# Four transformer layers on one core: normalised rows written on VectorE, a retimed small-head attention, and extra matmuls at its start

## The chip, the cores and the metric

The kernel runs on one core of a Trainium2 chip, as one launch. The metric is the device time of that launch in microseconds (us). TensorE (PE in the rows; PEld is its weight load), VectorE (DVE), ScalarE (ACT), GpSimd (POOL) and SyncE (SP, which only issues DMAs here) run side by side and wait for each other through semaphores. Each engine takes its own instructions strictly in program order.

## The reference

A state x of 16 sequences, 256 tokens and 128 channels passes through four attention and four feed-forward parts. After each part the state is added and normalised over the channels:

```python
x = _layernorm(x + _L0_attn_ref(x, ...))   # 16 heads of 64, inner norm
x = _layernorm(x + _L0_ffn_ref(x, ...))    # top-1 experts, fixed capacity
x = _layernorm(x + _L1_attn_ref(x, ...))   # softmax(-distance(q, k)), 16 heads of 8
x = _layernorm(x + _L1_ffn_ref(x, ...))    # top-2 experts, one mean weight per expert
x = _layernorm(x + _L2_attn_ref(x, ...))   # grouped projections, 16 heads of 8
x = _layernorm(x + _L2_ffn_ref(x, ...))    # MLP with weights +1 and -1
x = _layernorm(x + _L3_attn_ref(x, ...))   # causal, 16 heads of 8
x = _layernorm(x + _L3_ffn_ref(x, ...))    # top-2 experts with capacity, and a shared one
```

In `_L1_ffn_ref` each expert's output is multiplied by `mean_w`, the mean of the pair weights of the tokens that chose it, so it is one number for an expert. `_L2_attn_ref` and `_L3_attn_ref` are ordinary softmax attention with 8 channels a head; the third layer's is causal.

## The kernel before

The whole state stays on chip in `x_state` (128 partitions, 32 tiles of 128 channels); a batch is one sequence, that is two tiles (`TB` = 2), and there are 16 batches. The eight parts run one after another with a barrier between them. Three functions matter here:

- `attention_wide` is layer 0, `attention_dist` is layer 1, and `attention_small` is run twice, for layer 2 (not causal) and for layer 3 (causal).
- `routed_layer` is the expert part of layers 0, 1 and 3. It leaves its rows in a DRAM tensor, `results`. The attention of the next layer fetches them ("get", GpSimd indirect DMAs, one for a tile and expert), adds them to x ("join"), takes the moments ("stats"), forms 1/sqrt(var + eps) on GpSimd ("root") and writes the normalised rows into `x_state` (`write_last`).
- `sign_mlp` is the feed-forward part of layer 2. It leaves its sum on chip, so that layer 3's attention has no gathers; its join is one GpSimd addition (`join_acc`).

All attention functions share one schedule: a loop over slots, written out by hand in every engine's program. Slot s starts head s of the 256 (16 batches of 16 heads). Work on batch b is placed at an offset: `at(s, X_AT)` is true in slot 16 b + X_AT. Slots are only an order of instructions on each engine. In a slot of `attention_small` TensorE does `score(s)` (one head's scores, into one of two PSUM banks), then `score_turned(s - 30)` (the same scores transposed, with the negated maximum of each row added by three extra rows), then, twice in four slots, `weigh` (four heads' probabilities times values). VectorE does `row_max(s)`; the score of head n waits until the maximum of head n - 2 is taken. ScalarE does `exps(s - 30)`.

Around that, once a batch: X_AT = -35 transposes x, QK_AT = -33 projects q and k, `split_qk` (GpSimd) cuts them into three bf16 parts, V_AT = -29 projects v and starts `stack` on SyncE (two stores to DRAM, then six loads that spread the parts over partitions for all 16 heads). `score` of a batch's first head waits for these loads. After the last head come `turn_o` (slots OT_AT = 54 to 57), `normalise`, `turn_on`, `project_out` (Y_AT = 63), `norm_stats`, `root_var`, `write_x` and then `turn_new`, which transposes the finished rows (F_AT).

In the kernel before, `attention_small` gets its rows far ahead (GET_AT = X_AT - 35), joins at X_AT - 18, takes stats at X_AT - 17 and roots at X_AT - 15. Both normalised writes, `write_last` and `write_x`, are ScalarE activations, and as these take scale and bias, GpSimd also forms shift = -mean times rstd (two more small instructions, lines 674/676 and 701/703):

```python
nc.gpsimd.tensor_tensor(rstd[:], veps[:], mhalf[:], ALU.pow)
nc.gpsimd.tensor_tensor(shift[:], mv[:, :, 0], rstd[:], ALU.mult)
nc.gpsimd.tensor_scalar(shift[:], shift[:], -1.0, None, ALU.mult)
```

In `attention_dist`, `write_x` is two GpSimd instructions right behind the root (line 1231). In layer 1's `routed_layer` the mean weight of an expert is applied to each tile of rows as it leaves PSUM (`tile_mean`, line 2153), so that the join of layer 2 is two plain additions of 256 elements (line 1004).

Of the kernel before, what the change touches and what calls it, by code (L numbers as in the profile page):

```python
# [9 lines left out]
ALU = mybir.AluOpType  # L10
# [489 lines left out]
def attention_small(nc, name, x_state, consts, w, scratch, scale, causal, last, onward):  # L500
# [22 lines left out]
    with ExitStack() as ctx:  # L523
# [23 lines left out]
        shift, lshift = sb("shift", [P, TB]), sb("lshift", [P, 2, TB])  # L547
# [22 lines left out]
        JOINED = max(K, 1)  # L570
# [28 lines left out]
        with nc.Block() as block:  # L599
# [28 lines left out]
            def _(pool):  # L628
# [38 lines left out]
                def root_var(b):  # L667
                    pool.wait_ge(y_steps, 5 * (b + 1))
                    after(pool, x_done, TB * b)
                    nc.gpsimd.tensor_scalar(veps[:], mv[:, :, 1], EPS, None, ALU.add).then_inc(rooted, 1)  # L670
                    pool.wait_ge(rooted, 4 * b + 1)
                    nc.gpsimd.tensor_tensor(rstd[:], veps[:], mhalf[:], ALU.pow).then_inc(rooted, 1)
                    pool.wait_ge(rooted, 4 * b + 2)
                    nc.gpsimd.tensor_tensor(shift[:], mv[:, :, 0], rstd[:], ALU.mult).then_inc(rooted, 1)
                    pool.wait_ge(rooted, 4 * b + 3)
                    nc.gpsimd.tensor_scalar(shift[:], shift[:], -1.0, None, ALU.mult).then_inc(rooted, 1)
# [17 lines left out]
                def root_last(b):  # L694
# [3 lines left out]
                    pool.wait_ge(l_rooted, 4 * b + 1)  # L698
                    nc.gpsimd.tensor_tensor(lrstd[:, b % 2, :], lveps[:, b % 2, :], mhalf[:], ALU.pow).then_inc(l_rooted, 1)
                    pool.wait_ge(l_rooted, 4 * b + 2)  # L700
                    nc.gpsimd.tensor_tensor(lshift[:, b % 2, :], lmv[:, b % 2, :, 0], lrstd[:, b % 2, :], ALU.mult).then_inc(l_rooted, 1)
                    pool.wait_ge(l_rooted, 4 * b + 3)
                    nc.gpsimd.tensor_scalar(lshift[:, b % 2, :], lshift[:, b % 2, :], -1.0, None, ALU.mult).then_inc(l_rooted, 1)

                for s in range(FIRST, LAST + 4):
# [9 lines left out]
                    if (b := at(s, Y_AT + 4)) is not None:  # L715
                        root_var(b)
# [4 lines left out]
                    if (b := at(s, OT_AT - 4)) is not None:  # L721
                        add_out_bias(b)

            @block.tensor
            def _(pe):
                pe.wait_ge(loaded, LOADED)

# [114 lines left out]
                for s in range(FIRST, LAST + 4):  # L842
# [29 lines left out]
            def _(act):  # L872
# [46 lines left out]
                def write_last(b):  # L919
                    act.wait_ge(l_rooted, 4 * b + 4)  # L920
                    for tile in range(TB):
                        nc.scalar.activation(x_state[:, TB * b + tile, :], ly(b)[:, tile, :], ACT.Identity, bias=lshift[:, b % 2, tile:tile + 1],
                                             scale=lrstd[:, b % 2, tile:tile + 1]).then_inc(x_ready, 1)

                def write_x(b):
                    act.wait_ge(rooted, 4 * b + 4)
                    for t in range(TB):
                        nc.scalar.activation(x_state[:, TB * b + t, :], y[:, t, :], ACT.Identity, bias=shift[:, t:t + 1], scale=rstd[:, t:t + 1]).then_inc(x_done, 1)

# [27 lines left out]
            def _(dve):  # L957
# [40 lines left out]

                def join_rows(b):
                    dve.wait_ge(fetched[b % 2], 16 * TB * K * (b // 2 + 1))  # L1000
                    after(dve, x_ready, TB * (b - 1))
                    for k in range(K):
                        after(dve, joined_x, K * b + k if k else 0)
                        nc.vector.tensor_tensor(ly(b), lrows[:, b % 2, :, k, :], ly(b) if k else x_state[:, TB * b:TB * (b + 1), :], ALU.add).then_inc(joined_x, 1)
# [14 lines left out]
                for s in range(FIRST, LAST + 9):  # L1019
                    if K and (b := at(s, JOIN_AT)) is not None:  # L1020
                        join_rows(b)
                    if (b := at(s, STATS_AT)) is not None:
                        stats_last(b)
                    if (n := head(s)) is not None:
# [7 lines left out]
                    if onward["gate"] is not None and (b := at(s, LG_AT)) is not None:  # L1032
# [3 lines left out]
def attention_dist(nc, name, x_state, consts, w, scratch, last, onward):  # L1036
# [24 lines left out]
    with ExitStack() as ctx:  # L1061
# [85 lines left out]
        with nc.Block() as block:  # L1147
# [37 lines left out]
            def _(pool):  # L1185
# [42 lines left out]
                def write_x(b):  # L1228
                    pool.wait_ge(rooted_var, 2 * b + 2)
                    for t in range(TB):  # L1230
                        nc.gpsimd.tensor_scalar(x_state[:, TB * b + t, :], y[:, t, :], mv[:, t, 0:1], rstd[:, t:t + 1],
                                                ALU.subtract, ALU.mult).then_inc(x_done, 1)

# [28 lines left out]
                for s in range(FIRST, LAST + 8):  # L1262
# [16 lines left out]
                    if (b := at(s, Y_AT + 3)) is not None:  # L1279
                        root_var(b)  # L1280
                        write_x(b)
# [247 lines left out]
            def _(dve):  # L1529
# [52 lines left out]

                def stats_last(b):
# [12 lines left out]
                for s in range(FIRST, LAST + 8):  # L1596
# [12 lines left out]
                    if (b := at(s, Y_AT + 2)) is not None:  # L1609
                        norm_stats(b)  # L1610


def routed_layer(nc, layer, x_state, consts, w, dram, held, XT):
# [17 lines left out]
    with ExitStack() as ctx:  # L1631
# [60 lines left out]
        if mean2:  # L1692
            wsum, mean, silus = sb("wsum", [P, E]), sb("mean", [P, E]), sb("silus", [P, 2, F])
            tile_mean, meant = sb("tile_mean", [P, Q]), sem("meant")
# [49 lines left out]
        with nc.Block() as block:  # L1744
# [226 lines left out]
            def _(dve):  # L1971
# [109 lines left out]
                def mean_weights():  # L2081
# [4 lines left out]
                    link(nc.vector.tensor_tensor(past[:], numbers[:, 0:E].unsqueeze(1).to_broadcast([P, Q, E]),  # L2086
                                                 tile_of[:].unsqueeze(2).to_broadcast([P, Q, E]), ALU.is_equal))
                    link(nc.vector.tensor_tensor(past[:], past[:], mean[:].unsqueeze(1).to_broadcast([P, Q, E]), ALU.mult))
# [421 lines left out]
```

## Time and profile before

| | |
|---|---|
| median of 3 runs | 2958.49 us (2956.53 to 2959.1) |
| the profiled execution | 2959.1 us, of which the span of instructions is 2957.3 us |
| busy share of the span | PE 80%, PEld 56%, DVE 49%, ACT 50%, POOL 45% |
| mean granted TensorE clock | 0.875 of full |
| layer 2 attention, first to last write | 1641.6 to 2043.4 us |
| layer 3 attention, first to last write | about 2231 to 2582.6 us |

The granted clock has two levels, 0.50 (1.2 GHz) and 1.00 (2.4 GHz); a window with a value between them holds some of both. Times of instructions are counted in us from the first instruction. The profile is of one execution, so its own time, 2959.1 us, is the one that the rows add up to.

### The profile page before, as it was taken

The page shows a single profiled execution, that of the slowest core. Times are in us where ns is not written, and L with a number is a line of the kernel's source. Part 1 is how long each engine was busy: PE and PEld are TensorE (multiplying, and loading weights), DVE is VectorE, ACT ScalarE, POOL GpSimd, SP SyncE. Part 2 cuts the span into 40 slices and gives each one's busy share as a digit, 9 for nine tenths or more (in the row PEclk, how much of TensorE's full clock was granted, in tenths as well). Part 3 has the DMA queues.
Part 4 walks back from the last instruction along what each step waited for, and adds up shares of the span by engine and source line. Part 5 has one row for each costly group of instructions (what it writes and reads, how often), then busy time and mean ns, then how long its engine had stood idle before and what let it go on. Part 6 is the DMA issues. An engine that isn't in the chain of part 4 may idle for free. (4 is left out here: it accounts for less than half of the span.)

```text
span 2957.3 us, 52459 instructions
## 1 busy us (share of the span) xinstructions
PE 2353.9 (80%) x17870; PEld 1649.4 (56%) x17870; DVE 1451.2 (49%) x4042; ACT 1478.2 (50%) x3688; POOL 1331.2 (45%) x2068
## 2 busy tenths in 40 slices
PE   6999999994667999970699499996996999835860
PEld 4666666663654666540699245553553777524750
DVE  3555555553116999962233356672003566330753
ACT  4666666662336999960122146674221666511421
POOL 2444444444227888635433546531003454253255
PEclk9999999997776999995799558898995999977975
DMA  3000000002113222103111233320002322020212
GB/s 135 1 1 1 1 1 1 1 1 77 64 56 96 73 73 72 50 8 118 50 44 48 81 94 86 90 69 8 0 0 75 105 89 88 4 73 32 80 64 61
DMA packets 100387, 153.42 MB, mean 52 GB/s; under 512 B 16850, under 2 KB 69988, under 8 KB 93092
## 3 DMA queue, kind: packets, MB, share of 16 engines
q1 hardware_dynamic: 88356, 128.32, 13.7%
q0 software_dynamic: 11776, 21.81, 2.4%
q8 instruction: 146, 2.39, 0.3%
q14 instruction: 109, 0.89, 0.1%
HBM read 99.85 MB, written 48.24 MB: 50 GB/s over the span
## 5 line engine op out<-in xcount | busy, mean ns | idle before, releaser
L970 DVE TENSOR_REDUCE A_nmax<-A_S 128x2 f32<-128x512 f32 (+1 forms) x512 | 310.5, 621 | 227.8 <-PE A_S L760 110.6
L181 POOL TENSOR_SCALAR A_prob<-A_prob,A_rinv 128x256 f32<-128x256 f32 x512 | 235.4, 478 | 371.1 <-DVE A_rinv L433 371.1
L901 ACT ACTIVATE A_PT<-A_E 128x512 f32<-128x512 f32 (+1 forms) x512 | 275.3, 546 | 163.9 <-PE A_E L777 78.9
L428 DVE TENSOR_REDUCE A_nmax<-A_S 128x2 f32<-128x512 f32 x256 | 164.8, 685 | 160.9 <-PE A_S L271 160.9
L371 ACT ACTIVATE A_prob<-A_S,A_nmax 128x256 f32<-128x256 f32 x512 | 234.8, 477 | 4.9 <-DVE A_nmax L428 4.9
L1787 POOL COPY L_wr<-L_w 128x1024 f32 (+1 forms) x144 | 104.1, 725 | 242.5 <-PE L_k L1861 125.5
L1780 POOL DMA_INDIRECT sent<-x_state,row x160 | 154.6, 966 | 118.5 <-DVEq L2036 70.7
L1552 DVE TENSOR_SCALAR_CACHE_REDUCE A_D<-A_S 128x256 f32<-128x256 f32 x512 | 193.5, 417 | 16.8 <-PE A_S L1335 16.6
L1558 DVE COPY A_PT<-A_T 128x512 f32<-128x512 f32 x256 | 175.2, 687 | 19.3 <-PE A_T L1348 18.8
L1348 PE MATMUL A_T<-ident_sb,A_D 128*128 128x128 f32 x1024 | 161.3, 281 | 27.1 <-ACT A_D L1477 14.5
L1954 ACT ACTIVATE L_silus<-L_k 128x512 f32<-128x512 f32 x72 | 43.0, 597 | 262.7 <-PE L_k L1857 262.7
L1871 PE MATMUL L_k<-L_w,L_hT 128*128 (+1 forms) x1184 | 162.7, 275 | 0.8 <-ACT L_hT L1959 0.7
L254 PE MATMUL A_M<-A_xT,A_wqk 128*128 128x256 f32 x512 | 143.5, 403 | 22.3 <-ACT A_xT L357 16.2
L793 PE MATMUL A_O<-A_PT,A_v 128*32 128x256 f32 (+1 forms) x2048 | 160.4, 387 | 0.0
L384 ACT ACTIVATE A_OT<-A_O,A_bv 128x256 f32<-128x256 f32 x128 | 60.6, 474 | 191.0 <-PE A_O L299 191.0
L1348 PEld LDWEIGHTS A_T<-ident_sb,A_D 128*128 128x128 f32 x1024 | 117.5, 143 | 56.8 <-ACT A_D L1477 22.7
L1871 PEld LDWEIGHTS L_k<-L_w,L_hT 128*128 128x128 f32 x1184 | 147.0, 192 | 1.6 <-issue 1.1
L1840 PE MATMUL L_k<-ident_sb,L_xe 128*128 128x128 f32 x184 | 29.3, 287 | 147.2 <-DMA L_xe<-sent 146.2
L271 PE MATMUL A_S<-A_QK 64*128 64x256 f32 x1024 | 146.1, 404 | 0.0
L1213 POOL TENSOR_TENSOR A_D<-A_D 128x1024 f32<-128x1024 f32 x64 | 120.7, 1892 | 47.5 <-ACT A_D L1472 47.3
L299 PE MATMUL A_O<-A_PT,A_V 128*64 128x256 f32 x1024 | 138.8, 392 | 0.8 <-ACT logit L394 0.8
L284 PEld LDWEIGHTS A_T<-ident_sb,A_prob 128*128 128x128 f32 x1024 | 117.4, 141 | 37.2 <-issue 34.5
(380 smaller groups left out, 6024.2 us busy)
## 6 DMA issues: line engine op xcount, KB each, us to landing
A_QS<-stack_q SPq DMA_DIRECT2D x144, 192.0 KB
A_KS<-stack_k SPq DMA_DIRECT2D x144, 192.0 KB
L_xe<-sent SPq DMA_DIRECT2D x46, 256.0 KB
results<-L_ye SPq DMA_DIRECT2D x46, 256.0 KB
stack_q<-A_parts SPq DMA_DIRECT2D x48, 192.0 KB
stack_k<-A_parts SPq DMA_DIRECT2D x48, 192.0 KB
L_w<-f_w SPq DMA_DIRECT2D x24, 256.0 KB, 10.4
sent<-A_zeros SPq DMA_DIRECT2D x9, 512.0 KB
```

Of the source, the lines that this page charges most:

```text
L181: nc.gpsimd.tensor_scalar(prob[:, n % NP, j, t, :], prob[:, n % NP, j, t, :], rinv[:, n % NP, j, t:t + 1], 1.0, ALU.mult, ALU.mult).then_i ...
L271: i = nc.tensor.matmul(psS[n % 2][j][:, t, :], QK[rows, n % NQ, 0, t * P:(t + 1) * P], QK[rows, n % NQ, 1, :], start=True, stop=True)
L371: nc.scalar.activation(prob[:, n % NP, j, t, :], psS[n % 2][j][:, t, :], ACT.Exp, bias=nmax[:, n % NP, j, t:t + 1], scale=1.0, accum_out=r ...
L428: nc.vector.tensor_reduce(nmax[:, n % NP, j, :], psS[n % 2][j][:], AX.X, ALU.max, negate=True).then_inc(maxed, 1)
L793: i = nc.tensor.matmul(psO[32 * j:32 * (j + 1), 0, n0:], v1[:, b % NV, m, h, :], p, start=(m == 0), stop=(m == TB - 1), skip_group_check=True)
L901: nc.scalar.activation(PT[:, n % RING, :], psE[n % 2][:, 0:BLOCKS, :].rearrange("p a b -> p (a b)"), ACT.Exp, scale=scale).then_inc(expd, 1)
L970: nc.vector.tensor_reduce(nmax[:, b % 2, :, h], view, AX.X, ALU.max, negate=True).then_inc(maxed, 1)
L1348: i = nc.tensor.transpose(T[:, m, t * P:(t + 1) * P], D[:, u % RD, c:c + P], consts["ident"][:])
L1552: nc.vector.tensor_scalar(D[:, u % RD, c:c + SEQ], psS[n % 2][:, t, :], 1e-12, None, ALU.max, ALU.min, accum_out=D[:, u % RD, W + TB * j + ...
L1558: nc.vector.tensor_copy(PT[:, n % RP], psT[n % 2][:]).then_inc(turned_v, 1)
L1780: pool.indirect_dma_start(sent, bass.IndirectOffsetOnAxis(ap=row[:, k, t:t + 1], axis=0), x_state[:, t, :], None).then_inc(sent_all, 16)
L1871: m = nc.tensor.matmul(psY[q % 2][:, k * P:(k + 1) * P], hT[:, i % HT, f, :], moving, start=(f == 0), stop=(f == NF - 1))
```

## The change

Five things are changed, and the rest is left alone:

1. In `attention_small` both normalised writes move from ScalarE to VectorE, as (y - mean) times rstd in one instruction a tile; the two shift instructions are gone from both roots on GpSimd.
2. The offsets of `attention_small` change: get X_AT - 19, join X_AT - 8, stats X_AT - 7, root X_AT - 5 in layer 2 (join X_AT - 15, stats X_AT - 10 in layer 3), `turn_new` two slots earlier, logits one.
3. TensorE gets `keep_busy`: a bf16 matmul of identity by identity, 128 x 128 weights and 512 columns, into a PSUM bank that nobody reads then: one in each slot from -8 to 29, four in each slot from 30 to 33. That is 54 in each of layers 2 and 3.
4. Layer 1's expert weight is no longer applied to the tiles; it is put into `weight` for each token and pair, and the join of layer 2 becomes four VectorE instructions (row times weight plus sum, 128 elements each) in place of two additions.
5. In `attention_dist` `write_x` moves from GpSimd to VectorE, four slots later.

```diff
-    F_AT, LG_AT = Y_AT + 11, Y_AT + 13
+    F_AT, LG_AT = Y_AT + 9, Y_AT + 12
-    GET_AT, NORM_AT = X_AT - 35, X_AT - 15
-    JOIN_AT, STATS_AT = (X_AT - 18, X_AT - 17) if last["K"] else (X_AT - 21, X_AT - 17)
+    GET_AT, NORM_AT = X_AT - 19, X_AT - 5
+    JOIN_AT, STATS_AT = (X_AT - 8, X_AT - 7) if last["K"] else (X_AT - 15, X_AT - 10)
-        JOINED = max(K, 1)
+        JOINED = TB * K if K else 1
 # attention_small, GpSimd: root_var (root_last likewise)
-                    nc.gpsimd.tensor_tensor(shift[:], mv[:, :, 0], rstd[:], ALU.mult).then_inc(rooted, 1)
-                    nc.gpsimd.tensor_scalar(shift[:], shift[:], -1.0, None, ALU.mult).then_inc(rooted, 1)
-                    if (b := at(s, Y_AT + 4)) is not None:
-                        root_var(b)
...
+                    if (b := at(s, Y_AT + 3)) is not None:
+                        root_var(b)
 # attention_small, TensorE
+                def keep_busy(times):
+                    for _ in range(times):
+                        nc.tensor.matmul(psB[:], consts["identb"][:], consts["identb"][:].unsqueeze(1).to_broadcast([P, 4, P]),
+                                         start=True, stop=True, skip_group_check=True)
...
+                    if -8 <= s < LAG_E:
+                        keep_busy(1)
+                    if LAG_E <= s < LAG_E + 4:
+                        keep_busy(4)
 # attention_small, ScalarE
-                def write_last(b):
-                    act.wait_ge(l_rooted, 4 * b + 4)
-                    for tile in range(TB):
-                        nc.scalar.activation(x_state[:, TB * b + tile, :], ly(b)[:, tile, :], ACT.Identity, bias=lshift[...], scale=lrstd[...])
-                def write_x(b): ...
-                    if (b := at(s, NORM_AT + 4)) is not None:
-                        write_last(b)
-                    if (b := at(s, Y_AT + 9)) is not None:
-                        write_x(b)
 # attention_small, VectorE (write_last the same with lmv, lrstd)
+                def write_x(b):
+                    dve.wait_ge(rooted, 2 * b + 2)
+                    for t in range(TB):
+                        nc.vector.tensor_scalar(x_state[:, TB * b + t, :], y[:, t, :], mv[:, t, 0:1], rstd[:, t:t + 1],
+                                                ALU.subtract, ALU.mult).then_inc(x_done, 1)
-                        nc.vector.tensor_tensor(ly(b), lrows[:, b % 2, :, k, :], ly(b) if k else x_state[...], ALU.add).then_inc(joined_x, 1)
+                        for tile in range(TB):
+                            nc.vector.scalar_tensor_tensor(out=ly(b)[:, tile, :], in0=lrows[:, b % 2, tile, k, :],
+                                                           scalar=last["weight"][...], in1=ly(b)[:, tile, :] if k else x_state[...],
+                                                           op0=ALU.mult, op1=ALU.add).then_inc(joined_x, 1)
+                    if (b := at(s, NORM_AT + 2)) is not None:
+                        write_last(b)
+                    if (b := at(s, Y_AT + 8)) is not None:
+                        write_x(b)
 # attention_dist: write_x leaves GpSimd (behind root_var at Y_AT + 3), VectorE gets
+                    if (b := at(s, Y_AT + 7)) is not None:
+                        write_x(b)
 # routed_layer of layer 1, VectorE: mean_weights and take_y
-                    link(nc.vector.tensor_tensor(past[:], numbers[...], tile_of[...], ALU.is_equal))
-                    link(nc.vector.tensor_tensor(past[:], past[:], mean[...], ALU.mult))
-                    nc.vector.tensor_reduce(tile_mean[:], past[:], AX.X, ALU.add).then_inc(meant, 1)
+                    for k, sel in enumerate((sel1, sel2)):
+                        link(nc.vector.tensor_tensor(d[:], sel[:], over_t(mean), ALU.mult))
+                        link(nc.vector.tensor_reduce(weight[:, k, :], d[:], AX.X, ALU.add))
-                        i = nc.vector.tensor_tensor(ye[...], by_tile(psY[q % 2]), tile_mean[...], ALU.mult)
+                        i = nc.vector.tensor_copy(ye[:, q % 2, :, :], by_tile(psY[q % 2]))
```

## Rows read from the trace of the kernel before

**Rows 1.** The page, part 2: granted TensorE clock in 40 equal slices.

```profile
PEclk9999999997776999995799558898995999977975
```

**Rows 2.** Windows: length; busy (count) of PE, PEld, DVE, ACT, POOL; clock; DMA; GB/s.

```profile
1718.40:1771.90 53.50, 53.50 (x278) 27.87 (x277) 25.33 (x48) 26.35 (x56) 21.62 (x35) 0.50 0.30 92
...
1806.90:1902.50 95.60, 88.05 (x660) 49.52 (x660) 58.48 (x130) 60.77 (x137) 52.61 (x96) 0.82 0.29 84
...
2264.40:2294.00 29.60, 27.59 (x160) 18.32 (x160) 18.54 (x41) 6.10 (x17) 12.76 (x23) 0.50 0.35 108
...
2327.00:2509.00 182.00, 182.00 (x2227) 138.78 (x2225) 110.54 (x301) 120.69 (x314) 88.77 (x180) 1.00 0.30 92
...
958.30:1252.40 294.10, 271.52 (x2400) 180.88 (x2396) 282.89 (x1137) 293.06 (x510) 234.79 (x259) 1.00 0.23 68
```

**Rows 3.** Windows of `row_max` (line 970), layers 2 and 3: its busy time, count, clock.

```profile
1702.70:1718.40 15.70, 10.57 (x16) 0.50 0.38 119
1718.40:1771.90 53.50, 22.02 (x32) 0.50 0.30 92
...
1771.90:1806.90 35.00, 18.64 (x28) 0.99 0.35 94
...
1895.70:1902.50 6.80, 3.37 (x5) 0.50 0.22 77
1902.50:1939.50 37.00, 20.50 (x31) 1.00 0.31 88
...
2327.00:2509.00 182.00, 86.74 (x159) 1.00 0.30 92
```

**Rows 4.** Timeline of TensorE, two stretches of layer 2: start, duration, line.

```profile
1719.58 0.63 PE L763 MATMUL A_S<-A_KS,A_QS 72*128 72x256 bf16 x2
...
1720.43 0.63 PE L763 MATMUL A_S<-A_KS,A_QS 72*128 72x256 bf16 x2
...
1923.99 0.39 PE L763 MATMUL A_S<-A_KS,A_QS 72*128 72x256 bf16 x2
...
1924.45 0.38 PE L763 MATMUL A_S<-A_KS,A_QS 72*128 72x256 bf16 x2
```

**Rows 5.** Timeline of layer 2, a join on VectorE and TensorE behind it.

```profile
1935.18 0.42 DVE L1004 TENSOR_TENSOR A_lsum<-A_lrows,A_lsum 128x256 f32<-128x256 f32 x1
...
1936.27 0.39 PE L763 MATMUL A_S<-A_KS,A_QS 72*128 72x256 bf16 x2 [0.82 <-DVE A_nmax L970]
```

**Rows 6.** Timeline, four other stretches: row writes and weighted additions by engine.

```profile
122.59 0.60 DVE L477 TENSOR_SCALAR x_state<-A_s,A_mv,A_rstd 128x128 f32<-128x128 f32 x2 [0.89 <-POOL A_rstd L196]
...
1321.10 1.58 POOL L1231 TENSOR_SCALAR x_state<-A_y,A_mv,A_rstd 128x128 f32<-128x128 f32 x2
...
2041.75 0.88 ACT L928 ACTIVATE x_state<-A_y,A_shift,A_rstd 128x128 f32<-128x128 f32 x2 [4.19 <-POOL A_shift L676]
...
2857.80 2.32 DVE L2168 SCALAR_TENSOR_TENSOR L_y<-L_rows,weight,L_y 128x128 f32<-128x128 f32 x8
```

**Rows 7.** Timeline, start of layer 2 attention.

```profile
1654.51 0.30 DVE L1013 BATCH_NORM_AGGREGATE A_lmv<-A_lstats 128x2 f32<-128x6 f32 x2
...
1656.95 0.27 POOL L697 TENSOR_SCALAR A_lveps<-A_lmv 128x2 f32<-128x2 f32 x1
...
1658.38 0.25 POOL L703 TENSOR_SCALAR A_lshift<-A_lshift 128x2 f32<-128x2 f32 x1
...
1658.76 0.88 ACT L922 ACTIVATE x_state<-A_lsum,A_lshift,A_lrstd 128x128 f32<-128x128 f32 x2 [15.92 <-POOL A_lshift L703]
...
1660.18 0.95 POOL L687 DMA_INDIRECT A_lrows<-results,row  x1 [0.30 <-issue]
...
1663.03 0.84 ACT L886 ACTIVATE A_qk<-A_X,A_bqk 128x256 f32<-128x256 f32 x2 [2.17 <-PE A_X L740]
...
1665.28 0.77 POOL L640 CAST A_parts<-A_qk 128x512 bf16<-128x512 f32 x1
```

**Rows 8.** Groups of VectorE by line and form in 958.3 to 1252.4.

```profile
L1568 DVE TENSOR_TENSOR A_On<-A_B,A_rinv 128x128 f32<-128x128 f32 x12 | 3.5, 292 | 0.4
```

More of the change, by code:

```diff
@@ L917, in take_max @@
                     nc.scalar.activation(nmT[:, b % 2, :], psA[:].rearrange("p a b -> p (a b)").bitcast(BF16)[0:PARTS * H, 0:SEQ], ACT.Copy).then_inc(nm_ready, 1)
-                def write_last(b):
-                    act.wait_ge(l_rooted, 4 * b + 4)
-                    for tile in range(TB):
[L922 to L928, printed above, removed]
                 def take_new(b):
@@ L1002, in join_rows, with write_last @@
                     for k in range(K):
-                        after(dve, joined_x, K * b + k if k else 0)
-                        nc.vector.tensor_tensor(ly(b), lrows[:, b % 2, :, k, :], ly(b) if k else x_state[:, TB * b:TB * (b + 1), :], ALU.add).then_inc(joined_x, 1)
+                        after(dve, joined_x, JOINED * b + TB * k if k else 0)
+                        for tile in range(TB):
+                            nc.vector.scalar_tensor_tensor(out=ly(b)[:, tile, :], in0=lrows[:, b % 2, tile, k, :],
+                                                           scalar=last["weight"][:, k, TB * b + tile:TB * b + tile + 1],
+                                                           in1=ly(b)[:, tile, :] if k else x_state[:, TB * b + tile, :],
+                                                           op0=ALU.mult, op1=ALU.add).then_inc(joined_x, 1)
+                def write_last(b):
+                    dve.wait_ge(l_rooted, 2 * b + 2)
+                    for tile in range(TB):
+                        nc.vector.tensor_scalar(x_state[:, TB * b + tile, :], ly(b)[:, tile, :], lmv[:, b % 2, tile, 0:1], lrstd[:, b % 2, tile:tile + 1],
+                                                ALU.subtract, ALU.mult).then_inc(x_ready, 1)
                 def stats_last(b):
@@ L1031, in _ @@
                         norm_stats(b)
-                    if onward["gate"] is not None and (b := at(s, LG_AT)) is not None:
+                    if (b := at(s, Y_AT + 8)) is not None:
+                        write_x(b)
+                    if onward["gate"] is not None and (b := at(s, LG_AT + 1)) is not None:
                         take_logits(b)
@@ L1226, in root_var @@
                     nc.gpsimd.tensor_tensor(rstd[:], veps[:], mhalf[:], ALU.pow).then_inc(rooted_var, 1)
[L1228 to L1232, printed above, removed]
                 def get_last(b, i):
@@ L1280, in _ @@
                         root_var(b)
-                        write_x(b)
             @block.tensor
@@ L1581, in norm_stats, with write_x @@
                         nc.vector.bn_aggr(mv[:, t, :], stats[:, t, :]).then_inc(y_steps, 1)
+                def write_x(b):
+                    dve.wait_ge(rooted_var, 2 * b + 2)
+                    for t in range(TB):
+                        nc.vector.tensor_scalar(x_state[:, TB * b + t, :], y[:, t, :], mv[:, t, 0:1], rstd[:, t:t + 1],
+                                                ALU.subtract, ALU.mult).then_inc(x_done, 1)
                 def stats_last(b):
```

19 lines of the change are left out of this document (2 added, 17 removed).

## The prediction

> **What bounds the kernel now.** I read four views, from the whole to one slot. The clock line of the page [rows 1] comes first: outside feed-forward parts TensorE is at full clock in most slices, but not where layer 2's attention runs (1641.6 to 2043.4, its slices 23 to 28) nor where layer 3's begins. The windows [rows 2] say what a low clock costs there. In 1718.4 to 1771.9 TensorE is busy for 53.50 of 53.50 us at 0.50: it is the bound, and at half speed. The windows of `row_max` [rows 3] count heads, one for each: 32 heads in those 53.5 us, 1.67 each, against 28 in 35.0 and 31 in 37.0 at full clock, 1.22 on the mean. Layer 3, full clock without a break and TensorE busy 182.00 of 182.00 [rows 2], has 159 heads in 182.0 [rows 3], 1.145 a head or 18.3 a batch. Between 1806.9 and 1902.5 the clock falls four times (mean 0.82); the last of them shows 5 heads in 6.8 [rows 3].
>
> The timeline [rows 4] checks this on one instruction: the two matmuls of a `score` take 0.63 at half clock and the next pair that follows starts 0.85 later (1719.58 to 1720.43), 0.39 and 0.46 at full (1923.99 to 1924.45). In both gaps lie two 256-column score matmuls and two of the same size for `score_turned`, so a 512-column matmul, half of that, costs 0.43 at half and 0.23 at full clock.
>
> Why full clock here needs 1.22 a head and not 1.145 is in [rows 5]: once a batch VectorE has a clump (normalise, a join of two additions of 0.42, stats), the row maxima come late, and TensorE stands for 0.82 before a score. Layer 1's steady part is bound elsewhere: ScalarE busy 293.06 of 294.10, VectorE 282.89 [rows 2].
>
> **The change, part by part.** The sum is made against the profiled execution, 2959.1; the median is 0.6 below it.
>
> *Prices.* Two row writes cost VectorE 0.60 (seen in layer 0), GpSimd 1.58 and ScalarE 0.88 [rows 6]. Eight weighted additions of 128 elements take 2.32, so four take 1.2, against 0.84 for the two additions in the join of layer 2 [rows 5, 6]. The second shift instruction takes 0.25, and the write follows 0.38 behind its start; with the first of about the same size they cost some 0.6 [rows 7].
>
> *Layer 2, start: -3.8.* Moments of batch 0 are ready at 1654.81, but the root starts at 1656.95 because GpSimd first issues the gets of batch 1. Then come two shifts, the write (1658.76), and before `split_qk` of batch 0 (1665.28) the gets of batch 2, the root of batch 1 and its shifts, although ScalarE had q and k ready at 1663.87 [rows 7]. By the new offsets the root of batch 0 (slot -40) stands ahead of the gets of batch 1 (-38 to -35), and `split_qk` (-30) right behind these; the gets of batch 2 and the second root (-24) come later. So: moments 1654.81 plus 0.36 for the longer join, root 1.1 and write 0.60 give rows at 1656.9 instead of 1659.64, and q and k at about 1661.2; four gets at 1.25 (0.95, and 0.30 between them) from 1656.4 end at 1661.4. The split starts about 1661.5, 3.8 earlier. Bounds: 0 (a transfer takes it back) to -5.
>
> *Layer 2, the slow stretch: -17.7.* From slot -8 on there is a keep_busy in every slot, and four in each of slots 30 to 33, the slots in which `score_turned` and `weigh` begin. I take it that the clock rises in the ramp or with these, as it rises by itself at 1771.9, when the ends of batches (turn_o and the rest) come to TensorE in addition. The ramp's batches are paced by something else: 16 heads in 15.7 [rows 3], at half clock and yet 0.98 a head, since only scores run and the stack's loads release them; that stays. So 53.5 us become one batch at 15.7 (still waiting for its stack) and one at layer 3's pace, 18.3: 34.0, -19.5. The single keep_busy of the ramp lie in waits for the stack or behind VectorE's 0.69 per head. Of the sixteen in slots 30 to 33, half are hidden by the same waits and eight lie on the path at full clock: 8 x 0.23 = +1.8. Together -17.7. Bounds: 0, if the clock stays, to -21.
>
> In sentences by themselves: the Trainium skill (page "TensorE: Matmul & The Clock Gate", section "Part 1: The HAM clock gate") says that throttled is the default and that sustained activity of TensorE releases it. The trace agrees in part only: the engine is recorded busy for 53.50 of 53.50 us at 0.50 [rows 2]. If what the page calls activity were this record of busy time, keep_busy would add nothing to a stretch so full, and the sum would be 17.7 longer, 2942. If it is something that more matmuls add to, the sum stands. The row speaks for neither; the case without a lift is a rival below.
>
> *Layer 2, 1771.9 to 1939.5: -10.* It holds 167.6 us and, with the counts of [rows 3], about 130 heads: 1.29 each. At 1.22 they would take 158.6 (-9.0), at 1.145, with no stalls, 148.9 (-18.7). The clock dips lie behind the VectorE clump. The new order splits it: join at slot 5 of 16, stats 6, `write_x` 7, `write_last` and `normalise` 10 (modulo the batch), so that the longest addition to a slot is 1.2 to 1.3, not the 2.5 of three neighbours. Against it, VectorE gets 1.56 us a batch (0.60 + 0.60 + 0.36), GpSimd's root must be done before slot 10 (by the schedule it has 0.8 us to spare), and nothing fills TensorE here. I take -10, about half-way; bounds 0 to -20. What is behind a late `write_x` on VectorE is the next `row_max`, and TensorE's score waits for that.
>
> *Ends.* Layer 2's last rows: shifts and ScalarE's write (1.45 together) become a write of 0.60: -0.9; the last ScalarE write there came 4.19 after its predecessor, so it is on the path [rows 6]. Layer 3's last rows the same, -0.9. Layer 1: GpSimd's 1.58 becomes 0.60, -1.0 [rows 6].
>
> *Layer 3.* Start: two shifts gone and 0.88 to 0.60, -0.8. The clock is 0.50 to 2294.0, and there are no gathers; 32 heads in that stretch with TensorE busy 27.59 of 29.60 [rows 2], the batches 14.8 apart, faster than 18.3, because no second half of a head's work is yet due. Half the sixteen keep_busy on the path +1.8, an earlier rise -0.5: +1.3 (bounds 0 to +3.2). The steady 182.0 do not move: TensorE is never idle, VectorE is busy for 110.54 and takes 1.2 a batch more.
>
> *Layer 1, steady: 0.* VectorE is idle for 11.2 of 294.1, twelve batches [rows 2, 8], 0.93 a batch; the new write needs 0.60. It fits if it falls in the gaps, and ScalarE stays the bound. The most that it can cost is 0.60 x 16 = +9.6. The edits to the weights in layer 1's experts put two products and two sums on VectorE while GpSimd sends, and a copy of the same size for a product: 0.
>
> *Sum:* -3.8 - 17.7 - 10 - 0.9 - 0.9 - 1.0 - 0.8 + 1.3 = -33.8. That is 2925.3 for the profiled execution, and 2924.7 against the median. With the dips at 0 or -20, and the start, keep_busy and layer 1 at half their bounds, the forecast's own band is 2910 to 2940.
>
> **The rivals.**
>
> - *The clock rises and falls again.* In the third and fourth batch join and stats come before turn_o adds to TensorE's work, nothing keeps it busy from slot 34 on, and the clock goes back to 0.50 until about 1771.9. For it: in the trace it falls four times after having risen [rows 2, 3]. Against it: those fall behind a clump that is now split. The slow stretch then gives some 2 instead of 17.7, and the dips -2 of -10: 2924.7 + 16 + 8 = 2949.
> - *keep_busy doesn't do what it is for.* The clock stays low until 1771.9, and 54 matmuls at 0.43, some 16 on the path in the two layers, cost 7. For it: 53.50 busy of 53.50 did not lift the clock. Left are the start (3.8), the ends and layer 3's start (3.6), and some 3 of the dips: 2958.5 - 3.8 - 3.6 - 3 + 7 = 2955.
> - *VectorE becomes the bound: slower.* It gets 0.60 x 16 = 9.6 in layer 1, 1.56 x 16 = 25 in layer 2, and 1.20 x 16 = 19 in layer 3, 54 us in all. It matters if the writes delay `row_max`: in layer 2 each score waits for one (0.82 in [rows 5]), and in layer 1 only 0.93 a batch is free. For it: the waits of [rows 5] are there now. Against it: layer 3's TensorE has no idle time, and VectorE is busy for 61% there. It decides the sign when over 34 of the 54 lie on the path; a typical case, layer 1 and 2 in full and half of layer 3 (44), gives 2924.7 + 44 = 2969, all of it 2979.
>
> **How the numbers follow.** Forecast 0.62, the clock falls again 0.17, no lift 0.07, VectorE 0.14. A difference of 0.2% (5.9 us) is about what a measurement of this kernel tells from no change. Faster by more than that (below 2952.6): the forecast's 0.62, of the second case 0.13 and of the third 0.02, 0.77. Slower (above 2964.4): 0.13. The rest, 0.10, within. The range goes from 2908, below the forecast's band, to 2954, which takes in the clock falling again and half of no lift, and leaves VectorE's case and some 0.05 out.
>
> **What would show it.** Granted clock 1.00 from about 1720 in layer 2 and no window at 0.50 with dense work; the heads of `row_max` at 18.3 a batch there; `split_qk` of batch 0 some 4 us nearer to the layer's start; no 0.82 waits of TensorE on `row_max` in each batch; layer 1's window with ScalarE at 99% and its length unchanged; layer 3 equally long to 1 or 2 us. It is wrong if clock is 0.50 somewhere in 1720 to 1940 of layer 2 for over 10 us, if VectorE releases ScalarE or TensorE more often in layer 1, or if GpSimd's root comes after slot 10 and VectorE waits for it in each batch.

## The result, and the profile after

The changed kernel took 2983.1 us against 2957.5 before: ratio 1.0091 (95% interval 1.0072 to 1.0109), slower by 26 us where I forecast 34 less. The profiled executions, 2957.3 and 2989.0 us of span, are 31.7 apart. Counted by the first and the last `row_max` of each small attention: up to layer 2's first -2.9, layer 2's 16 batches +28.5 (318.4 to 346.9), the way to layer 3's first -0.9, layer 3's batches +1.2, and the rest +5.8, in a part of which only layer 3's last rows have changed code. The loss is in layer 2: its first two batches +3.4, the third and fourth -8.4, the fifth to twelfth +30.4, the last four +3.0.

In the diff of the section on the change, the lines under "attention_small, ScalarE" (`write_last`, `write_x` and their two calls) are marked as added; the change removes them.

Windows of the kernel after, for layer 2's third and fourth batch together, and the fifth to twelfth (columns as in [rows 2]):

```profile
1719.10:1764.20 45.10, 42.75 (x287) 22.52 (x284) 26.95 (x56) 24.45 (x52) 20.28 (x29) 0.74 0.33 95
1764.20:1962.20 198.00, 166.80 (x1250) 93.44 (x1248) 126.59 (x296) 103.29 (x225) 95.36 (x148) 0.84 0.27 76
```

and the same two stretches of the kernel before:

```profile
1718.50:1772.00 53.50, 53.50 (x279) 27.84 (x276) 25.33 (x48) 26.35 (x56) 21.62 (x35) 0.50 0.30 92
1772.00:1939.60 167.60, 153.79 (x1250) 87.75 (x1248) 110.01 (x248) 111.95 (x256) 95.69 (x169) 0.90 0.31 87
```

The first stretch became 8.4 us shorter and its clock rose to 0.74, about half of what I forecast for `keep_busy`. That it is not `keep_busy`'s doing in this kernel is shown by e1 below. The second holds the same 1250 TensorE instructions and became 30.4 longer. TensorE is busy 13.0 longer (the mean clock fell from 0.90 to 0.84), and idle 31.2 in place of 13.8. The dips of [rows 1] have not gone. A slice of the page after spans three batches; the clock record of the trace shows one fall in each of the eight, 64 us at 0.50 together, for five falls and 35 us in the same batches of the kernel before.

```profile
PEclk9999999996867999985899687898997999967975
```

One batch shows the idle part. VectorE, TensorE and GpSimd around head 10 of the tenth batch (b = 9), kernel after, three timelines:

```profile
1901.60 0.69 DVE L956 TENSOR_REDUCE A_nmax<-A_S 128x2 f32<-128x512 f32 x1 [0.66 <-PE A_S L760]
1902.21 0.60 DVE L1005 TENSOR_SCALAR x_state<-A_lsum,A_lmv,A_lrstd 128x128 f32<-128x128 f32 x2
1904.58 0.69 DVE L956 TENSOR_REDUCE A_nmax<-A_S 128x2 f32<-128x512 f32 x1 [1.78 <-PE A_S L760]
```

```profile
1902.27 0.38 PE L760 MATMUL A_S<-A_KS,A_QS 72*128 72x256 bf16 x2
1902.49 0.38 PE L777 MATMUL A_E<-A_QS,A_KS 75*128 75x256 bf16 x2
1902.71 0.38 PE L760 MATMUL A_S<-A_KS,A_QS 72*128 72x256 bf16 x2
1902.93 0.38 PE L777 MATMUL A_E<-A_QS,A_KS 75*128 75x256 bf16 x2
1905.33 0.39 PE L760 MATMUL A_S<-A_KS,A_QS 72*128 72x256 bf16 x2 [2.02 <-issue]
```

```profile
1899.98 1.08 POOL L682 DMA_INDIRECT A_lrows<-results,row  x1 [0.20 <-issue]
1901.36 0.96 POOL L682 DMA_INDIRECT A_lrows<-results,row  x1 [0.30 <-issue]
1902.63 1.00 POOL L682 DMA_INDIRECT A_lrows<-results,row  x1 [0.30 <-issue]
1903.93 0.94 POOL L682 DMA_INDIRECT A_lrows<-results,row  x1 [0.30 <-issue]
```

The first of the two scores in the TensorE rows is head 10's, recorded at 1902.27 to 1902.65; the second is head 11's. The `row_max` of head 10, with nothing before it on VectorE since 1902.81, starts at 1904.58: 1.9 us after the recorded end of its score. (Ends of matmuls are modelled; the release shows when it was really done.) GpSimd issues the four gets of a later batch from 1899.98 to 1904.87. From the fifth batch to the twelfth, VectorE is idle for 3.37, 2.11, 3.37, 1.81, 2.20, 1.78, 2.17 and 1.81 us before this `row_max`. In six of them it starts within 0.4 us of the end of the last get, in the fifth and the seventh 1.2 us behind it.

The thirteenth batch is the comparison that this trace holds itself. Its join, root, both row writes, turn_o and turn_new stand where they stood, and the gets alone are missing, since no batch is left to fetch:

```profile
1975.50 0.59 DVE L1005 TENSOR_SCALAR x_state<-A_lsum,A_lmv,A_lrstd 128x128 f32<-128x128 f32 x2
1976.27 0.69 DVE L956 TENSOR_REDUCE A_nmax<-A_S 128x2 f32<-128x512 f32 x1 [0.17 <-PE A_S L760]
```

Head 10 is on time. The trace of before has the same late head 10, which I hadn't looked for: an idle time of 1.10 to 1.37 us in the fifth to eleventh batch, against 0.69 in the twelfth, the first without gets, so it is late by 0.4 to 0.7. There the `row_max` starts 1.9 to 2.8 us before the last get ends.

### The profile page after: what moved, and what is told of

Same layout as the page of the kernel before. It is cut to its first block and busy times, and to the rows that moved or that the text cites. A ratio compares the mean times of both kernels' runs of the same rounds, so it can differ in the third digit from the quotient of the medians.

```text
span 2989.0 us, 52579 instructions
## 1 busy us (share of the span) xinstructions
PE 2366.8 (79%) x17978; PEld 1651.6 (55%) x17978; DVE 1513.0 (51%) x4235; ACT 1441.0 (48%) x3560; POOL 1281.6 (43%) x1908
## 3 DMA queue, kind: packets, MB, share of 16 engines
q1 hardware_dynamic: 88356, 128.32, 13.8%
## 5 line engine op out<-in xcount | busy, mean ns | idle before, releaser
L760 PE MATMUL A_S<-A_KS,A_QS 72*128 72x256 bf16 x512 | 113.4, 308 | 38.9 <-DVE A_nmax L956 25.7
```

## The experiments

Medians of different chips can't be compared here: the kernel before itself took 2957.5 and 2960.7 us in the first two sets and 2896.9 in the next, where no head is late. Each ratio below is against the kernel before on the same chip. Executions on a 2960 chip also spread (the kernel before took 2944.6 to 2978.7 us in 28 on one of them), and a trace is one execution: e4's is the shortest of its ten (2954.0, median 2970.1), e3's is longer than its median (2963.7, 2955.6). So small differences between windows of two traces there prove little. "A 2960 chip" and "a 2895 chip" name the two kinds. "Eight batches" is layer 2's fifth to twelfth, from first `row_max` to first `row_max`, the same work in each trace.

### A 2960 chip

**e1_no_keep**

```diff
-                    if -8 <= s < LAG_E:
-                        keep_busy(1)
-                    if LAG_E <= s < LAG_E + 4:
-                        keep_busy(4)
```

> The changed kernel without the 108 keep_busy matmuls. Changed kernel 2983.1, kernel before 2957.5. If keep_busy does what I took it for (it lifts the clock in layer 2's ramp, which in the changed kernel is 5 us shorter up to the fifth batch), leaving it out costs 5 to 15: 2988 to 2998, and the clock stays at 0.50 up to about 1770. If its matmuls only cost time, 2976 to 2981. Neither explains the 25.6 us alone: in both theories below the steady batches of layer 2 stay at 24 to 25 us.

Measured: 1.0094 (1.0061 to 1.0127), eight batches 198.5 us, as with keep_busy, and the third and fourth together 43.4, against 45.1 with it. The clock rose at 1720, not at 1770: the rest of the change lifts it as far alone. keep_busy is not the loss, and no gain can be seen from it in this kernel.

**e2_old_offsets**

```diff
-    GET_AT, NORM_AT = X_AT - 19, X_AT - 5
-    JOIN_AT, STATS_AT = (X_AT - 8, X_AT - 7) if last["K"] else (X_AT - 15, X_AT - 10)
+    GET_AT, NORM_AT = X_AT - 35, X_AT - 15
+    JOIN_AT, STATS_AT = (X_AT - 18, X_AT - 17) if last["K"] else (X_AT - 21, X_AT - 17)
```

> The changed kernel with the offsets of before for get, join, stats and root (turn_new stays two slots earlier). Theory A, the order: the stand of TensorE at head 10 of each batch comes from gets, row write and turn_new lying together late before the batch; then the steady batches of layer 2 fall from 24.8 to some 21, and the time to 2955 to 2965. Theory B, VectorE's added work (two row writes and four contended weighted additions a batch) sets the pace wherever it stands: 2978 to 2986, steady batches 24 or more.

Measured: 1.0044 (1.002 to 1.0068), eight batches 186.3. In between: the old offsets give back about half of the loss. VectorE is idle for 1.59 to 1.92 us before head 10 in the batches with gets and for 0.69 in the next one, and the clock falls once in each of seven batches.

**e3_keep_only**, the kernel before with the lines that e1 removes and the function `keep_busy` itself.

> The kernel before with keep_busy added and nothing else. If the clock follows it: full clock in the ramp from about 1700 and the 53.5 us of the slow stretch down by 10 to 18, so 2940 to 2950. If it does nothing for the clock: 2958 to 2964. Theories A and B say nothing different here; it sizes the one gain that I forecast as the largest.

Measured: 0.9973 (0.9946 to 1.0001), so a gain of the whole kernel is not clear of the spread. Windows of the third and fourth batch, and the eight behind them:

```profile
1723.10:1757.90 34.80, 32.28 (x286) 18.16 (x284) 24.39 (x48) 25.04 (x56) 21.07 (x33) 1.00 0.43 123
1757.90:1936.90 179.00, 162.85 (x1250) 94.09 (x1248) 110.40 (x249) 113.19 (x257) 96.96 (x173) 0.84 0.30 86
```

The slow stretch went from 53.5 at 0.50 to 34.8 at 1.00, -18.7 where I had worked out -17.7. But 11 of them are given back in the eight batches: from the sixth on the clock falls once in each, the seventh to eleventh take 23.8 to 24.2 us, with nothing added to VectorE, and the idle time before head 10 is 1.03 to 1.43 us (once 2.35) for 0.69 without gets.

**e4_turn_late**

```diff
-    F_AT, LG_AT = Y_AT + 9, Y_AT + 12
+    F_AT, LG_AT = Y_AT + 11, Y_AT + 13
```

> The changed kernel with turn_new and the logits two slots (one slot) later, as before. If the early turn_new, two transposes at slot 8 just ahead of the stand at head 10, is what makes the stand (a part of theory A): the stand falls from 2 us towards the 0.5 of the kernel before and the time to 2960 to 2970. If not: 2980 to 2986. Theory B expects no change.

Measured: 1.0025 (0.9998 to 1.0052). Windows, the eight batches:

```profile
1754.90:1925.40 170.50, 144.73 (x1250) 84.15 (x1248) 126.82 (x296) 102.33 (x225) 95.17 (x148) 0.96 0.31 90
```

My expectation had the reason wrong and the time nearly right. Head 10 is still late (2.03 to 2.42 us of idle time on VectorE), and TensorE is idle for 25.8. What went in this execution is the clock's fall behind it: 12.9 us at 0.50 for 64, a mean of 0.96 for 0.84, and TensorE busy 22 us less. So the late head costs some 2 a batch, and the half clock that may follow it costs more than the head itself. The traced execution is 16 us below the median, so a typical one may hold more falls; that the time improved is shown by the ratio, against 1.0094 for e1, the other kernel of this set with the new order.

### 2895 chips

**e5_gets_at_14** (`GET_AT = X_AT - 15`)

> The changed kernel with the four gets of a batch in slots 14, 15, 0 and 1 of the 16 in place of 10 to 13 (GET_AT = X_AT - 15). In both kernels row_max of head 10 comes late exactly in the batches that have gets (0.5 us in the kernel before, 2 to 3.4 after). Theory G: the issue of the gets on GpSimd is what holds TensorE up; the late head moves to 14 or 15 and head 10 is on time; the ratio to before moves either way by what lies in those slots (0.998 to 1.009). Theory O: it is TensorE's own work of slots 6 to 9 (turn_o, turn_new, weigh) and the late head stays 10; ratio 1.007 to 1.011.

**e6_scalar_writes**

```diff
+                    if (b := at(s, NORM_AT + 4)) is not None:
+                        write_last(b)          # ScalarE, with lshift from GpSimd
+                    if (b := at(s, Y_AT + 9)) is not None:
+                        write_x(b)             # ScalarE, with shift from GpSimd
```

> The changed kernel with both row writes of attention_small back on ScalarE with their shifts, and turn_new two slots later, as there (so it is compared with e4_turn_late, ratio 1.0025). If VectorE's writes are a cost of layer 2: ratio 0.995 to 0.999 and the batches under 20.5 us. If the writes cost nothing where they stand: 1.001 to 1.004.

**e7_plain_join**

```diff
-                        for tile in range(TB):
-                            nc.vector.scalar_tensor_tensor(out=ly(b)[:, tile, :], ...)
+                        nc.vector.tensor_tensor(ly(b), lrows[:, b % 2, :, k, :], ly(b) if k else ..., ALU.add).then_inc(joined_x, 1)
```

> The changed kernel with the expert weights applied to the tiles as before and the join of layer 2 in two plain additions of 256 elements. The four weighted additions take 2.3 us a batch in the trace of the changed kernel (first two 0.78 each, beside GpSimd), the two plain ones 0.85. If that is on the path: 16 x 1.4 = 22 us less, ratio 1.001 to 1.003. If it is hidden: 1.007 to 1.010.

**e8_old_order**, the edits of e2 and e4 together.

> The changed kernel with the offsets of before for get, join, stats, root and with turn_new two slots later: the whole order of before, with keep_busy, VectorE's writes and the weighted join left in. Singly the two gave ratios of 1.0044 and 1.0025 against 1.0091. If they are two causes: 0.997 to 1.000. If either alone takes away the same stand: 1.002 to 1.004. If VectorE's load is a cause beside the order it stays above 1.000, since keep_busy alone gives 0.997.

Measured: e5 0.9964 (0.9949 to 0.9979), e6 0.9982 (0.9964 to 0.9999), e7 0.9943 (0.9924 to 0.9962), e8 0.9983 (0.9963 to 1.0004). Head 10 is not late in any of the four traces; their eight batches take 148.2, 146.5, 145.1 and 151.5 us. The expectations had been written against ratios of a 2960 chip. For the change's own ratio on this kind it had to be run there.

**r1_after, r1_before, r1_gets_at_14, r1_plain_join**: the changed kernel, the kernel before, and e5 and e7 again, side by side.

> The changed kernel itself, on the chip of this set. The chips differ: the kernel before took 2957.5 and 2960.7 on two of them, 2896.9 on the third, and on the third no kernel had a late row_max at head 10. Theory C, the late head is a state of the chip, and the change loses only there: where before takes some 2897, this one has even batches of 18.5 in layer 2 and a ratio of 0.994 to 0.999; where before takes some 2960, the late head of 2 to 3 us, batches of 24 to 25 and a ratio of 1.007 to 1.011. Theory O (TensorE's own work in slots 6 to 9) expects the late head on every chip.

> The kernel before itself, for its trace on the chip of this set. Ratio 1.000. Theory C: on a chip of some 2897 layer 2's attention is about 30 us shorter than the 318 us from first to last row_max, with no late head; on one of 2960 as in the trace before, late by 0.5 at head 10.

> The changed kernel with the gets in slots 14, 15, 0, 1 (run before on the fast chip only, 0.9964). On a chip with the late head, theory G (the gets hold TensorE up) expects it to move to head 14 or 15, and a ratio of 0.998 to 1.006; if the head stays 10, the gets are not what holds it. On a chip without it, 0.996 again.

> The changed kernel with the two plain additions (0.9943 on the fast chip). On a chip with the late head: VectorE's share of the loss is what this one gives back against the changed kernel of the same set; hidden 0 to 0.001, on the path 0.005 or more. On one without it 0.994 again, and the changed kernel itself 0.003 to 0.004 above.

Measured on a 2895 chip: the change 0.9971 (0.9954 to 0.9988), the kernel before 1.0002 (0.9982 to 1.0023), gets at 14 0.9981 (0.9963 to 1.0), plain join 0.9951 (0.9935 to 0.9967). So here the change is faster by 0.3%. The trace of r1_before is one of the short executions (2884.5, median 2893.4), so against r1_after's (2883.2, median 2883.6) it hides most of this. Windows of r1_before, of r1_after and of r1_plain_join, again two and eight batches:

```profile
1716.90:1760.30 43.40, 42.45 (x278) 22.61 (x276) 24.97 (x48) 25.77 (x56) 20.89 (x32) 0.68 0.38 106
1760.30:1906.00 145.70, 135.23 (x1250) 81.63 (x1248) 109.66 (x248) 110.78 (x257) 96.41 (x173) 1.00 0.37 102
```

```profile
1719.60:1753.40 33.80, 32.04 (x286) 18.25 (x284) 27.47 (x56) 23.81 (x52) 20.22 (x29) 1.00 0.42 117
1753.40:1901.60 148.20, 138.75 (x1250) 81.15 (x1248) 126.00 (x296) 102.20 (x225) 94.39 (x145) 1.00 0.36 103
```

```profile
1715.30:1748.20 32.90, 32.04 (x286) 18.32 (x284) 26.28 (x53) 23.77 (x52) 20.58 (x29) 1.00 0.45 127
1748.20:1893.30 145.10, 137.59 (x1250) 81.17 (x1248) 124.14 (x280) 101.22 (x225) 95.93 (x145) 1.00 0.36 106
```

The two batches that were slow go from 43.4 to 33.8 (I had forecast 34.0 and 1.8 on top). The eight have no dip to lose, in either, and get 2.5 longer: 18.2 to 18.5 a batch. The plain join takes this back, 18.1. And r1_before, with the clump of [rows 5] in every batch, keeps the clock at 1.00 through all eight. The rows of the weighted addition in r1_after give its price (min, median and max in ns):

```profile
L997 DVE SCALAR_TENSOR_TENSOR A_lsum<-A_lrows,weight,x_state x32: 338/810/1318, 1654.2 to 1907.8; 128x128 f32<-128x128 f32 x32
L997 DVE SCALAR_TENSOR_TENSOR A_lsum<-A_lrows,weight,A_lsum x32: 337/348/1199, 1654.8 to 1908.9; 128x128 f32<-128x128 f32 x32
```

The first two of each join, which run while GpSimd works on `split_qk`, take 0.81 (median), not the 0.29 that I divided out of eight. And the same place as above, head 10 of a batch with gets, in r1_after, VectorE and GpSimd:

```profile
1839.61 0.60 DVE L1005 TENSOR_SCALAR x_state<-A_lsum,A_lmv,A_lrstd 128x128 f32<-128x128 f32 x2
1840.39 0.69 DVE L956 TENSOR_REDUCE A_nmax<-A_S 128x2 f32<-128x512 f32 x1 [0.17 <-PE A_S L760]
```

```profile
1839.05 0.96 POOL L682 DMA_INDIRECT A_lrows<-results,row  x1 [0.30 <-issue]
1840.31 0.95 POOL L682 DMA_INDIRECT A_lrows<-results,row  x1 [0.30 <-issue]
1841.57 0.94 POOL L682 DMA_INDIRECT A_lrows<-results,row  x1 [0.30 <-issue]
```

Here the `row_max` starts in the middle of the gets, 0.17 after VectorE is free.

### Are the gets what holds TensorE up?

**r2_gets_at_14, e9_gets_by_sync, e10_join_and_gets.** The edit of e9:

```diff
+                def get_last(b, i):            # in SyncE's program, gone from GpSimd's
+                    tile, k = divmod(i, K)
+                    after(sp, joined_x, JOINED * (b - 1))
+                    row = (K * (TB * b + tile) + k) * P
+                    sp.dma_start(lrows[:, b % 2, tile, k, :], last["results"][row:row + P, :]).then_inc(fetched[b % 2], 16)
```

> The changed kernel with the gets in slots 14, 15, 0, 1, for the third time, in the hope of a chip on which the kernel before takes some 2960. There theory G (GpSimd's issue of indirect DMAs holds TensorE up) expects head 10 on time, a late row_max at head 14 to 1, and a ratio of 0.998 to 1.006; if it is not the gets, head 10 stays late and the ratio is 1.007 to 1.011. On a chip of 2895: 0.996 to 0.998 as before.

> The changed kernel with the 64 gets of layer 2 taken from GpSimd: SyncE copies 128 consecutive rows in place of the gathered ones, at the same slots (it fetches other rows, so layer 2 and what follows is computed from other data). Theory G on a chip of 2960: no late head at all, even batches of 18 to 18.5 in layer 2, the ratio 0.98 to 0.99. If it is the transfer and not its issue by GpSimd, head 10 stays late. On a chip of 2895: 0.994 to 0.998, next to the changed kernel's 0.997.

> Plain additions and gets at slot 14 together, the rest as changed. On a chip of 2895: as e7, 0.994 to 0.996. On one of 2960, if plain additions free VectorE and the gets lie where TensorE has less to do: 0.985 to 0.998; by theory VectorE the additions alone give 0.005 there.

Measured, a 2895 chip again: 0.998 (0.9959 to 1.0), 1.0026 (1.0005 to 1.0047) and 0.9958 (0.994 to 0.9975). e9 loses at its start: its fourth batch takes 25.5, most of it at the half clock, and its eight batches 148.7; why the clock falls there isn't shown. e10, the plain join with the gets at slot 14, is the best order found, with e7, and has the same 145.1 for eight batches.

**e11_gets_by_turns**, and the same once more as **r2_gets_by_turns**:

```diff
+                        if (b := at(s, GET_AT + i)) is not None and b % 2 == 0:
+                            get_last(b, i)
+                        if (b := at(s, GET_AT + 4 + i)) is not None and b % 2 == 1:
+                            get_last(b, i)
```

> The changed kernel with the gets of even batches in slots 10 to 13 and those of odd batches in 14, 15, 0, 1. On a chip of 2960: theory G expects the late row_max at head 10 in every second batch and at head 14 to 1 in the others; if TensorE's own work makes it, head 10 is late in all. On a chip of 2895: no late head, ratio 0.996 to 0.999.

> The same as e11_gets_by_turns once more. On a chip of 2960: theory G expects the late row_max at head 10 in every second batch and at head 14 to 1 in the others; if TensorE's own work makes it, head 10 is late in all. On a chip of 2895: no late head, ratio 0.996 to 0.999.

Measured: e11 on a 2895 chip 0.9977 (0.9954 to 1.0001), no late head; r2 on a 2960 chip 1.0103 (1.0019 to 1.0187), head 10 late in every batch. That looks like a verdict against the gets, and is none. GpSimd has no instruction between slots 10 and 14, so the moved gets are issued at once after the root of slot 8 all the same. An odd batch, GpSimd and VectorE of r2_gets_by_turns:

```profile
1889.72 0.94 POOL L682 DMA_INDIRECT A_lrows<-results,row  x1 [0.30 <-issue]
1890.97 0.95 POOL L682 DMA_INDIRECT A_lrows<-results,row  x1 [0.30 <-issue]
```

```profile
1889.13 0.59 DVE L1007 TENSOR_SCALAR x_state<-A_lsum,A_lmv,A_lrstd 128x128 f32<-128x128 f32 x2
1891.80 0.69 DVE L958 TENSOR_REDUCE A_nmax<-A_S 128x2 f32<-128x512 f32 x1 [2.08 <-DMA A_KS<-stack_k]
```

The releaser that the last row names can't be it: the program lets `row_max` wait for its own score alone. In this trace the late `row_max` starts within 0.6 of the end of the fourth get in seven of the eight batches (1771.2 for 1771.6, 1796.7 for 1796.2, 1821.6 for 1821.9, 1847.0 for 1847.4, 1867.2 for 1867.6, 1891.8 for 1891.9, 1914.7 for 1914.9) and 1.2 before it in the last. So e5 and its repeats are the changed kernel in another spelling: on 2895 chips they have its 148.2 for eight batches.

**e12_half_by_sync**, the gets of odd batches on SyncE as in e9, those of even ones on GpSimd.

> The changed kernel with the gets of odd batches taken from GpSimd: SyncE copies 128 consecutive rows in their place (other rows than the gathered ones, so the data of layer 2 and on are others). Moving gets within GpSimd's program told nothing, since it has nothing between slots 10 and 14 and issues them at the same time. Here, on a chip of 2960, theory G expects a late row_max at head 10 in even batches only (those in which GpSimd issues) and a ratio of 0.99 to 1.005; if it is TensorE's own work or the transfer, head 10 is late in all. On a chip of 2895: no late head, 0.997 to 1.003.

Measured, a 2895 chip: 1.0001 (0.9971 to 1.0031), head 10 as in r1_after (0.17 to 0.18) in the eight batches.

No run without GpSimd's gets met a 2960 chip, but the traces say more than their runs. TensorE raises a semaphore 3648 times in each; when it does is recorded, and can be laid beside the modelled end of the matmul that raises it. Late by over 0.5 us are, in the kernel after, 102 of the 213 that end while GpSimd issues indirect DMAs (or within 0.35 us of one) and 4 of the other 3435; in the kernel before, 92 of 218 and 3 of 3430. On 2895 chips it is 1 of 267 and 0 of 3381 (r1_after), at most 2 in the other traces, and 15 of 250 in r1_before. It goes by the issue and not by the transfer: while packets of GpSimd's DMAs still move and it issues none, 2 of 152 are late in the kernel after. This is an observation in traces, not an experiment, but with the thirteenth batch it speaks against theory O and for theory G.

## Why the prediction was wrong

- **The failed step** is "Layer 2, 1771.9 to 1939.5: -10", with bounds of 0 to -20: it measured +30.4, and +2.5 on a 2895 chip. I took VectorE's clump for what makes TensorE stand and for what the dips lie behind, and left no room for a loss. The clump was split as I said. But r1_before has the same clump and no dip: clock 1.00 and 18.2 us a batch. The largest stand was another one, head 10 in the batches with gets: against a batch without them it is late by 0.4 to 0.7 us in the kernel before and by 1.6 to 3.2 after, and the clock falls behind it once in each batch. e4's trace separates the two: with the late head and hardly a fall 170.5, with both 198.0.
- **Order or VectorE's load?** The old offsets give back half (e2), the later turn_new two thirds of the ratio (e4), keep_busy nothing (e1). What makes head 10 later is not settled. e3, with the old order and no added VectorE work, is late by 0.3 to 0.7 (once 1.7), e2, with that work, by 0.9 to 1.2. That could be VectorE's part; it alone makes no late head, since the thirteenth batch has it too. Another reading was left untested: with the two shift instructions gone and `root_var` a slot earlier, GpSimd reaches the first get sooner. It starts 1.1 to 1.5 us before VectorE is free for head 10 in the kernel before and in e3, and 2.4 to 2.9 before in after, e1, e2, e4 and r2_gets_by_turns, the five that lose more there. ScalarE's writes (with their shifts) and the plain join, which would tell the two apart, were measured only where no head is late.
- **The slow stretch, -17.7.** Right in mechanism as far as e3's trace goes: -18.7, alone, of which 11.4 came back behind it. In the changed kernel it was -8.4 on a 2960 chip and -9.6 on a 2895 one, where the traced execution of before has 43.4 and not 53.5. And e1 shows that the rest of the change does this without `keep_busy`, so the sum gave one gain to the wrong part. Before it, the first two batches, which I took to stay, got 3.4 longer.
- **Layer 2's start, -3.8**: `split_qk` of batch 0 came 3.9 us nearer to the first join (1653.19 and 1665.28 before, 1651.88 and 1660.11 after), as worked out, but the first `row_max` only 2.9 earlier, and 0.4 later on a 2895 chip. **Ends, -2.8, and layer 3's start, -0.8**: -0.9 from layer 2's last to layer 3's first `row_max`; the rest can't be told apart from the 5.8 behind layer 3. **Layer 3, +1.3**: +1.2, and its steady batches 18.4 in both, as forecast.
- **Layer 1, steady: 0.** 24.88 a batch for 24.76, about +2 in all: the 0.60 did not quite fit into the 0.93.
- **Prices.** Two row writes 0.60, as taken. The weighted join 2.3, not 1.2: I divided a row of eight (2857.80) beside which GpSimd only issues gathers, and computes nothing. On a 2895 chip this is the 2.5 us of the eight batches, by r1_plain_join.
- **The rivals.** "VectorE becomes the bound" had the sign, by luck: its writes and joins cost 2.5 us of the eight batches where no head is late, and are not shown to make the 30.4; "the clock falls again" had the clock, but in the wrong batches and for 24 of the 58 us between forecast and result. None said that the loss depends on the chip.

## What to carry to other kernels

Before a clump is blamed for an engine's stand, list for each slot of the schedule how late the released instruction starts; the largest such wait may be one that no row of the costliest groups names. Where the clock dips once a period, the dips can cost more than the stand that they follow: look at what stands within the dip's few microseconds, and try moving that (two slots of turn_new: 1.0025 for 1.0091). A period at the end of a loop that lacks one of the steady ones' parts is a comparison that costs no run. Moving an instruction by slots moves it in time only if its engine has other work or a wait in between. And a verdict of under 1% may be that of a chip: run both kernels on a second one.

## What the runs showed of the hardware

The chips are of two kinds for the kernel before, 2938 to 2979 us and 2878 to 2902, with nothing between. Between its traces on the two kinds (before and r1_before, 2957.3 and 2882.7 us of span), 32.5 of the 74.6 us lie between layer 2's first and last `row_max`, and 39.9 behind layer 3's last. The latter difference is in the last layer, where GpSimd issues 64 sends one after another (0.96 each) while the shared expert is computed. Windows of the kernel before, while the sends are issued, on a 2960 chip and, as r1_before, on a 2895 chip:

```profile
2625.00:2684.00 59.00, 4.17 (x10) 1.48 (x9) 0.69 (x1) 0.00 (x0) 44.75 (x47) 0.60 0.15 52
```

```profile
2593.00:2650.00 57.00, 36.04 (x226) 27.75 (x224) 4.15 (x6) 12.18 (x18) 43.29 (x46) 0.85 0.15 52
```

GpSimd issues at the same rate in both. On the second chip TensorE, ScalarE and VectorE compute beside it (226 matmuls); on the first they stand (10 matmuls, no ScalarE instruction), though no wait of theirs is on GpSimd's sends. With the thirteenth batch and the late semaphores above it looks as if on such chips GpSimd's issue of indirect DMAs holds up TensorE's completions: they are late beside it and hardly anywhere else. That it is the cause is argued, not shown by an experiment: the runs that took the gets from GpSimd ran on the other kind. Why chips differ in this, no run tells.
